# A fused two-layer decoder on one core: another order for the small jobs that share the spare PSUM bank of the attention loop

## The reference, cut to what matters

```python
def _w8a8_linear(x, w, b):                 # x and w coded in steps of their maximum / 127
    qx, sx = _dyn_quant(x); qw, sw = _quant_weight(w)
    return jnp.einsum('bnc,oc->bno', qx, qw) * (sx * sw[:, 0]) + b
q = _w8a8_linear(layernorm(x), wq, bq)     # 256 queries a batch, 16 heads of 16
k = cond @ wk.T + bk                       # 512 context rows a batch
v = cond @ wv.T + bv
attn = softmax(q @ k.T / 4 + mask)
x = x + tanh(g) * _w8a8_linear(attn @ v, wo, bo)
# then per token: layernorm, gate logits over 60 experts, softmax, top 4, place in the expert's list
```

## Time and profile before

| | us |
|---|---|
| median of 3 runs | 633.57 |
| lowest, highest | 632.21, 637.43 |
| the profiled execution, its own time | 636.62 |
| its span in the profile | 634.7 |
| the attention loop with its last restore, in the profile | about 22 to 217 |

### The profile page before, as it was taken

One profiled execution on the slowest core, in us unless ns is written; L12 is line 12 of the kernel. 1 busy time (PEld: TensorE's weight loads), 2 busy tenths in 40 slices (PEclk: granted clock), 3 DMA queues, 4 the chain that ended last, 5 costly groups with the idle time before them and its releaser, 6 DMA issues. The chain is left out here.

```text
span 634.7 us, 11207 instructions
## 1 busy us (share of the span) xinstructions
PE 548.3 (86%) x3526; PEld 371.4 (59%) x3526; DVE 364.0 (57%) x1183; ACT 241.1 (38%) x478; POOL 225.9 (36%) x280
## 2 busy tenths in 40 slices
PE   3899999998799779899879999788999878659956
PEld 1566676675566554566657777565547445337734
DVE  6878687767886776157865555443265742215522
ACT  3378878776687412022213332222121341003320
POOL 2211023121036336323316777654032422743430
PEclk9989999998999889999979999999999958959987
DMA  8900910990001046359858999992520100928815
GB/s 294 312 35 3 288 36 3 340 340 2 1 3 71 19 133 215 105 170 277 279 182 265 294 289 269 244 237 79 201 68 1 69 2 9 318 89 297 302 61 172
DMA packets 61445, 101.13 MB, mean 159 GB/s; under 512 B 7881, under 2 KB 37373, under 8 KB 61264
## 3 DMA queue, kind: packets, MB, share of 16 engines
q1 hardware_dynamic: 53808, 87.47, 44.2%
q0 software_dynamic: 7584, 13.02, 5.9%
HBM read 70.25 MB, written 38.57 MB: 171 GB/s over the span
## 5 line engine op out<-in xcount | busy, mean ns | idle before, releaser
L625 POOL DMA_INDIRECT token_y<-stage,y_row x78 | 76.4, 980 | 117.4 <-ACT stage L1511 107.9
L1966 PE MATMUL bank<-stage 128*128 128x352 f32 x312 | 110.1, 477 | 5.8 <-DMA stage<-in_w 5.3
L845 DVE CUSTOM_DVE_ANT_0 stage<-bank,stage 128x512 f32<-128x512 f32 x128 | 80.8, 687 | 28.5 <-PE bank L1723 27.8
L1411 ACT ACTIVATE stage<-bank 128x512 f32<-128x512 f32 x128 | 73.8, 598 | 42.0 <-PE bank L1737 42.0
L1984 PE MATMUL bank<-stage,e_hT 88*128 88x256 f32 x312 | 81.7, 384 | 1.2 <-DVE e_hT L1195 1.0
L1737 PEld LDWEIGHTS bank<-ident,stage 128*128 128x128 f32 x512 | 57.2, 144 | 37.8 <-issue 30.7
L1501 ACT ACTIVATE e_act<-bank 128x176 f32<-128x176 f32 x78 | 24.8, 318 | 143.2 <-PE bank L1966 143.2
L1737 PE MATMUL bank<-ident,stage 128*128 128x128 f32 x512 | 73.5, 285 | 4.4 <-ACT stage L1411 4.1
L1984 PEld LDWEIGHTS bank<-stage,e_hT 88*128 88x128 f32 x312 | 59.8, 193 | 23.6 <-DMA stage<-in_w 1.6
L1869 PE MATMUL bank<-xnT,sh_in 128*128 128x512 f32 (+2 forms) x144 | 70.5, 645 | 2.4 <-issue 2.0
L1966 PEld LDWEIGHTS bank<-stage 128*128 128x128 f32 x312 | 54.7, 195 | 26.5 <-DVE stage L1180 5.1
(11 more groups left out here) (238 smaller groups left out, 717.0 us busy)
## 6 DMA issues: line engine op xcount, KB each, us to landing
stage<-in_w SPq DMA_DIRECT2D x30, 704.0 KB, 7.7
stage<-in_w SPq DMA_DIRECT2D x48, 352.0 KB, 4.1
stage<-sorted_x SPq DMA_DIRECT2D x39, 272.0 KB, 4.4
sorted_x<-zeros SPq DMA_DIRECT2D x4, 2040.0 KB, 13.1
extra_x<-zeros SPq DMA_DIRECT2D x4, 1088.0 KB, 12.2
stage<-token_y SPq DMA_DIRECT2D x8, 512.0 KB, 4.4
sorted_x<-zeros SPq DMA_DIRECT2D x4, 816.0 KB, 13.4
stage<-in_w SPq DMA_DIRECT2D x18, 176.0 KB
```

Of the source, the lines that this page charges most:

```text
L625: gp.indirect_dma_start(out=y_dram[y.n][:, :], out_offset=bass.IndirectOffsetOnAxis(y_row[:, t:t + 1], 0), in_=e_y[:, t % NY, :], in_offse ...
L845: V.tensor_tensor_reduce(out=z_sb[:, s % 2, j, :], in0=bank[j][:], in1=mask[:, b % 2, k // 4, :], scale=-1.0, scalar=BIG, op0=ALU.add, op1 ...
L1411: A.activation(pT[:, s % 2, j].rearrange("p t n -> p (t n)"), bank[4 + j % 2][:], ACT.Exp, scale=1.0 if j < ON_ACT else -1.0).then_inc(exp ...
L1966: last = M.matmul(bank[2 + u % 2][:, 0:2 * I_EXP], xgT[:, u, c, :], w13[:, u, c, :], start=(c == 0), stop=(c == CC - 1))
```

## The change

It writes the jobs of bank 7 in another order. First halves now hold, for k = 0 to 7: none, r1, lg, v0, q, op, r0, ps (all taken by VectorE); second halves: qt1, x, k0, cx, co, qt0, k1 (all taken by ScalarE), v1. VectorE's and ScalarE's chores move with them: `take_v(b, 1)` goes from the end of k = 7 to the front of the next batch's k = 0, logits from k = 4 to 2, softmax from 5 to 4, pick from 6 to 5, `finish(b, 0)` from 5 to 6. ScalarE's takes now all stand behind the step's last exponent. The scores of k = 2 have a wait of their own for the second half of the keys. In the tail, `co` goes ahead of `lg` of batch 2, which moves to bank 6.

```diff
-            here = [("k0", b + 1), ("qt1", b if b else B), ("k1", b + 1), ("r1", b - 1), ("v0", b + 1), ("x", b - 2), ("cx", b + 1),
-                    ("lg", b - 2), ("q", b + 1), ("co", b - 1), ("op", b - 1), ("r0", b), ("qt0", b + 1), ("ps", b - 2), ("v1", b + 1)]
+            here = [("qt1", b if b else B), ("r1", b - 1), ("x", b - 2), ("lg", b - 2), ("k0", b + 1), ("v0", b + 1), ("cx", b + 1),
+                    ("q", b + 1), ("co", b - 1), ("op", b - 1), ("qt0", b + 1), ("r0", b), ("k1", b + 1), ("ps", b - 2), ("v1", b + 1)]
...
-            if (j, b) == ("ps", B - 2):
+            if b == B - 2 and j in ("lg", "ps"):
                 return 6
...
                 if k == 0:
+                    if b:
+                        take_v(b, 1)
                     if b > 1:
                         moments_of_updated(b - 2)
                     weigh_context(b)
...
-                if k == 2 and b + 1 < B:
-                    take_v(b + 1, 0)
+                if k == 2 and b > 1:
+                    route_logits(b - 2)
                 if k == 2 and b:
                     scales_of_o(b - 1)
                     dve.sem_inc(scales_o, 1)
+                if k == 3 and b + 1 < B:
+                    take_v(b + 1, 0)
                 if k == 3 and b + 2 < B:
                     moments_of_next(b + 2)
-                if k == 4 and b > 1:
-                    route_logits(b - 2)
                 if k == 4 and b + 1 < B:
                     take_q(b + 1)
-                if k == 5:
-                    if b:
-                        take_output(b - 1, 4)
+                if k == 4 and b > 1:
+                    route_softmax(b - 2)
+                if k == 5 and b:
+                    take_output(b - 1, 4)
+                if k == 5 and b > 1:
+                    route_pick(b - 2)
+                if k == 6:
                     finish(b, 0)
-                    if b > 1:
-                        route_softmax(b - 2)
-                if k == 6 and b > 1:
-                    route_pick(b - 2)
                 if k == 7 and b > 1:
                     route_slots(b - 2)
-                if k == 7 and b + 1 < B:
-                    take_v(b + 1, 1)
...
+                if k == 2:
+                    pe.wait_ge(job_act, taken_count("k1", b))
...
-            turn_x(B - 2)
             up_shared(L0, 0)
+            turn_x(B - 2)
+            codes_o(B - 1)
             gate_logits(B - 2)
-            codes_o(B - 1)
             output(B - 1)
```

More of the change, by code:

```diff
@@ L322, in build @@
         for b in range(B):
-            here = [("k0", b + 1), ("qt1", b if b else B), ("k1", b + 1), ("r1", b - 1), ("v0", b + 1), ("x", b - 2), ("cx", b + 1),
-                    ("lg", b - 2), ("q", b + 1), ("co", b - 1), ("op", b - 1), ("r0", b), ("qt0", b + 1), ("ps", b - 2), ("v1", b + 1)]
+            here = [("qt1", b if b else B), ("r1", b - 1), ("x", b - 2), ("lg", b - 2), ("k0", b + 1), ("v0", b + 1), ("cx", b + 1),
+                    ("q", b + 1), ("co", b - 1), ("op", b - 1), ("qt0", b + 1), ("r0", b), ("k1", b + 1), ("ps", b - 2), ("v1", b + 1)]
             JOBS += [(j, c) for j, c in here if 0 <= c < B]
-        JOBS += [("r1", B - 1), ("x", B - 2), ("lg", B - 2), ("co", B - 1), ("op", B - 1), ("x", B - 1), ("lg", B - 1),
+        JOBS += [("r1", B - 1), ("x", B - 2), ("co", B - 1), ("lg", B - 2), ("op", B - 1), ("x", B - 1), ("lg", B - 1),
                  ("ps", B - 2), ("ps", B - 1)]
@@ L1425, in _ @@
                     centre(s + 1, range(2))
-                if k == 0 and more:
-                    take_k(b + 1, 0)
-                if k == 1 and more:
-                    take_k(b + 1, 1)
-                if k == 3 and more:
-                    take_codes("cx", b + 1, 0)
-                if k == 6 and more:
-                    take_qt(b + 1, 0)
                 exponent(s, 2)
@@ L1440, in _ @@
                     take_qt(b, 1)
+                if k == 1 and b > 1:
+                    take_xn(b - 2)
+                if k == 2 and more:
+                    take_k(b + 1, 0)
                 if k == 2 and b > 1:
-                    take_xn(b - 2)
+                    route_exp(b - 2)
+                if k == 3 and more:
+                    take_codes("cx", b + 1, 0)
                 if k == 4:
@@ L1446, in _ @@
                         take_codes("co", b - 1, QT)
-                if k == 4 and b > 1:
-                    route_exp(b - 2)
+                if k == 5 and more:
+                    take_qt(b + 1, 0)
+                if k == 6 and more:
+                    take_k(b + 1, 1)
             back(B - 1, 1)
@@ L1788, in _ @@
                 turn_z(s, 1)
-                if k == 0 and more:
-                    keys(b + 1, 0)
-                if k == 1 and more:
-                    keys(b + 1, 1)
-                if k == 2 and more:
+                if k == 1 and b:
+                    restore(b - 1, 1)
+                if k == 2 and b > 1:
+                    gate_logits(b - 2)
+                if k == 3 and more:
                     values(b + 1, 0)
-                if k == 3 and more:
-                    codes_x(b + 1)
                 if k == 4 and more:
@@ L1800, in _ @@
                     output(b - 1)
-                if k == 6 and more:
-                    turn_q(b + 1, 0)
+                if k == 6:
+                    restore(b, 0)
                 if k == 7 and b > 1:
@@ L1810, in _ @@
                     turn_q(b, 1)
-                if k == 1 and b:
-                    restore(b - 1, 1)
-                if k == 2 and b > 1:
+                if k == 1 and b > 1:
                     turn_x(b - 2)
-                if k == 3 and b > 1:
-                    gate_logits(b - 2)
+                if k == 2 and more:
+                    keys(b + 1, 0)
+                if k == 3 and more:
+                    codes_x(b + 1)
                 if k == 4 and b:
                     codes_o(b - 1)
-                if k == 5:
-                    restore(b, 0)
+                if k == 5 and more:
+                    turn_q(b + 1, 0)
+                if k == 6 and more:
+                    keys(b + 1, 1)
                 if k == 7 and more:
@@ L1908, in _ @@
             last.then_inc(seq_pe, 1)
+            up_shared(L0, 0)
             turn_x(B - 2)
-            up_shared(L0, 0)
+            codes_o(B - 1)
             gate_logits(B - 2)
-            codes_o(B - 1)
             output(B - 1)
```

## The result

| | before | after |
|---|---|---|
| median, us (20 runs each) | 632.36 | 639.16 |
| lowest, highest | 627.02, 643.43 | 633.71, 647.22 |
| ratio, 95% interval | | 1.0106, 1.0079 to 1.0133 |
| the profiled execution, its own time | 636.62 | 639.21 |
| its span | 634.7 | 637.4 |

The changed kernel is slower by about 1.1% (6.7 us by the ratio, 6.8 by the medians); the interval holds the 1% bound of the prediction. The profiled execution of before was 4.3 over its median of 20 runs and that of after stands on its median, so the two spans differ by less than the medians do. The batches are the better measure. They run from the start of one batch's step k = 0 to the next (batch 3 to the last restore); the tail runs from there to the first turn of a routed expert.

A forecast was written before the change was run, and what follows sets the result against it. TensorE's stream bounds the attention stage, stopped by other engines' taking of bank 7. Batches 0 to 3 and tail, 2.6+2.1+2.1-2.0-0.2 = +4.6 us, against the median 633.57 gave 638.2; 8-in-10 range 631.5 to 644.

The forecast's parts named there:

- Work that no longer hides: Per batch: keys jobs into second halves +1.4, coding of x +0.4, restore 1 into a first half -0.5; +1.3 us.
- Batch 0: Keys leaving first halves save 2.0; second halves cost 3.8, coding 0.4, wait at k=6 0.43; +2.6 us.
- Batch 2, k = 1: Turn of x newly waits in bank 7 for VectorE's finish: 2.9 us, bounds 1.7 and 3.5.
- Batch 2, k = 5: Turn of q waits 1.8 us for VectorE's copies of the output.
- Batch 2, k = 6: Keys 1 waits 1.9 us for finish, pick now following the output at k=5.
- k = 7: Batch 2: places no longer wait for pick; the values wait 0.3 us for places.
- The clock in batch 2: One fall of the clock expected, after the 2.9 us wait, losing 1.7 us.
- Batch 3: k=0 +0.35, k=1 wait +1.6, moved jobs -1.1 and -1.2, end -1.7 (0 to -3.1); -2.0 us.
- Tail: Coding of the output, ahead of the logits, no longer waits 0.5 for their copy; -0.2 us.
- the first (hand-overs covered): Rival: VectorE takes first-half jobs during turns and weighing, only the k=4 wait stays; 626.0 us, chance 0.08.
- The third (room in TensorE's stream): Rival: the 4.6 us lie in miscounted slack, so no change; 633.6 us, chance 0.15.
- The second (the clock falls at more places): Rival: shorter waits in batch 2, k=5 and 6, and batch 3, k=1 cost 1.7 each; 642.5 us, chance 0.22.

The follow-up runs named there:

- (5): Changed kernel with the second values job taken at the end of k = 7 and keys 0 back in the first half of k = 0; 632.96 us, ratio 0.9978.
- (7): Kernel before with keys 1 alone moved from the first half of k = 1 to the second half of k = 6; executed once, 637.53 us.
- (1): Changed kernel with VectorE's finish of restore 1 ahead of the scales of x at k = 1; 635.45 us, ratio 1.0063.
- (3): Changed kernel with the pick of the experts back at k = 6, behind finish of restore 0; 633.55 us, ratio 1.0042.
- (8): Changed kernel with GpSimd's root ahead of the eight scatters of batch 1's rows, behind the loop; 638.15 us, ratio 1.0039.
- (11): Changed kernel with VectorE's moments of batch 2's updated rows ahead of its last places chore; executed once, 640.88 us.
- (10): Kernel before with the changed kernel's tail order alone; executed once, 638.28 us.
- (4): Kernel before with VectorE taking the gate logits at the end of k = 3, not at k = 4; 629.39 us, ratio 0.9945.
- (6): (4) with, in k = 7, the values in the first half and places in the second; 627.01 us, ratio 0.9938.
- (9): (6) with the changed kernel's tail order and VectorE's moments of batch 2's updated rows ahead of its last places chore; 621.98 us, ratio 0.9840.
- (2): Changed kernel with the second values job taken by VectorE at the end of k = 7, as in the kernel before; 637.75 us, ratio 1.0142.

## Why the prediction was right, and where it was off

The direction came out by the steps given, and the time nearly (638.2, measured 639.16). Part of that nearness is luck: the 638.2 stands on a median of three runs that was 1.2 over that of 20. The difference itself was forecast at 4.6 and measured at 6.8, and the term that decided "within 1%" against "over 1%" is the one of batch 3 and the tail: 0.13 in the two profiles for the -2.2 of the forecast.

- *Work that no longer hides*, +1.3 a batch: right. Batch 1 came out at +2.00 for 2.1, its waits at 0.32, 0.57 and 0.38 for 0.33, 0.5 and 0.43. (5) isolates one keys job at 0.75, (7) at 0.68, for 0.7 worked out.
- *Batch 0*: +2.66 for +2.6. Keys 0 had cost nothing, as said: where it is gone, the scores of k = 1 wait 1.50 instead of 0.27.
- *Batch 2, k = 1*: 2.99 for 2.9. (1) confirms its cause: 1.45 of it is the scales of x in VectorE's queue.
- *Batch 2, k = 5*: mis-sized, 0.99 for 1.8. I took the softmax at 1.74 from the earlier trace rows; in after it took 1.10 (155.30 to 156.40). In before one small operation of it (L923) took 0.79 beside GpSimd's operation on 512 columns, in after 0.16. And the wait of 0.57 at k = 4, which my own sum had, delays TensorE and so shortens this wait; I had counted VectorE's lateness without it.
- *Batch 2, k = 6*: 2.14 for 1.9, by pick, as (3) shows by moving it. *k = 7*: 0.36 for 0.3. (The waits that the prediction lists for batch 2 add up to 7.73, not 7.8, which changes nothing.)
- *The clock in batch 2*: one fall, as forecast, but behind the 2.14 and not the 2.99. The sum was right, its reason half so.
- *Batch 3*: -0.90 for -2.0. The term "-1.7 (between 0 and -3.1)" is the one that failed. In after the last turns waited 2.78 for ScalarE, which waited for VectorE's last scoring (214.08, behind pick), where before had 0.84, 0.47 and 1.43 in three waits: 2.74 in all. The same wait changed its name, so the end of the range at 0 would have been right for it. By steps: k = 0 +0.37 (forecast +0.35), k = 1 to 3 +0.23 (+0.5), k = 5 -1.21 (-1.2), and from the first scores of k = 6 to the last restore -0.27 (14.11 before, 13.84 after), where -1.7 was forecast. And -0.27 was a good case: with the same order at this place it was 15.2 to 15.3 in (1), (8) and (11), whose batch 3 is 0.5 longer than before's and not shorter.
- *Tail*: -0.2 expected, +1.03. The order of TensorE gave -0.41 (10). What was missed is a chain that no step of mine named: VectorE's moments behind places, GpSimd's norm, eight scatters of 1.3 each in its queue, and the root behind them. I had written that what follows attention "starts from the last restore and the x rows after it"; the x rows hang on this chain, and in after it held the root 1.29 beyond its input. The chain starts from the moments and not from the last restore. So by these rows an earlier last restore alone, which is what the -2.0 of batch 3 was to give, would have been lost behind it for the most part.

Of the rivals, the first (hand-overs covered) falls by the waits of 4.5 and 2.9 in total. The third (room in TensorE's stream) falls for batch 1, which has no late engine: +2.00; in batch 2 of (7) there was such room, but beside waits and not in the stream as such. The second (the clock falls at more places) did not come in after's profile: two falls behind batch 0, as before. Which rival was nearest matters less than that the two large errors, batch 3 and tail, pointed the same way; they are one error seen twice.

## What to carry to other kernels

When engines hand one buffer to one another, order the jobs by when their taker is free; sorting them by taker (one engine in each half) puts the long ones where nothing hides them. Moving one late chore to where its engine is idle gave a gain where the whole reordering gave a loss ((4), 0.9945, against after, 1.0106). A gain in a loop must be followed to what starts behind it: half of (6)'s was lost in a wait for rows that VectorE and GpSimd make, and (9) brought it back with another order of the tail and one of VectorE's chores moved. And look at a kernel without the edit before an edit is given the credit: (1) had (8)'s tail without it.

## What was not expected of the hardware

The clock's fall behind a wait of 2 to 3 us is not a function of the wait. The same 2.45 was followed by a granted mean of 0.72 in before and by 1.00 in (7); the same 2.14 by 0.73 in after and by 1.00 in (1); the same 2.99 by 1.00 in after and by 0.58 in (3). Windows behind those waits in (7) and (3):

```profile
146.00:152.00 6.00, 5.42 (x70) 3.99 (x71) 4.27 (x15) 3.90 (x10) 0.00 (x0) 1.00 0.01 4
```

```profile
137.00:142.00 5.00, 5.00 (x27) 4.14 (x28) 3.31 (x10) 2.98 (x5) 0.61 (x1) 0.58 1.12 398
142.00:146.00 4.00, 4.00 (x42) 2.90 (x41) 1.49 (x5) 1.69 (x3) 2.00 (x4) 0.67 0.82 289
```

A fall costs 1.6 to 3.2 us (8.95 against 7.35, 9.94 against 6.73), so a single profile is uncertain by that much at each such wait. Two or three of them could make up much of the spread of the runs, 627 to 643 in before; that is an estimate, since each kernel has one profile. What decides it stays open. The wait at the end of batch 3 (2.77 to 2.80) was followed by a fall in all of after, (1), (8) and (11), of different lengths.

Small operations of VectorE beside GpSimd's: the cast of 16 values (L938) took 0.92 at 210.94 in after while GpSimd worked on 512 columns (L707 and L708, the latter 1.80 long), against 0.17 without such company, and 0.40 in batch 2. It fell into pick, before the last scoring of batch 3. It was 0.92 again in (1), (2), (5), (8) and (11), and 0.18 in (3), where it comes after GpSimd's two operations; there the second of them took 1.29 instead of 1.80. And the slow small operation ends when GpSimd's does: 211.86 and 211.81 in after, 161.68 and 161.65 in its batch 2, 158.59 and 158.57 for L923 in before. So these rows show the small operation held until GpSimd's is done. No experiment was made for it alone.
